# A feature-interaction network on one core: chunk 1's products, the weight splits and chunk 0's loads put in another order

## The reference

```python
prev = x
for k in range(3):
    z = jnp.einsum('bmd,bhd->bdmh', x, prev).reshape(b, D, m * h)
    t = jnp.einsum('bdc,co->bdo', z, ws[k]) + bs[k]
    t = jnp.transpose(t, (0, 2, 1))
    norm = jnp.sqrt(jnp.sum(t * t, axis=(-2, -1), keepdims=True))
    t = t / norm
    logit.append(t)
    prev = t
z = jnp.sum(jnp.concatenate(logit, axis=1), axis=-1)
...
h = jnp.maximum(h @ W_top1 + b_top1, 0.0)
h = jnp.maximum(h @ W_top2 + b_top2, 0.0)
y = h @ W_top3
```

## Time and profile before

| | |
|---|---|
| median of 3 runs | 1050.79 us |
| profiled execution | 1049.29 us |
| its span | 1047.5 us |
| granted TensorE clock, mean of the span | 1.0 |
| TensorE busy | 1019.5 us, 97% |
| VectorE busy | 967.0 us, 92% |
| GpSimd busy | 872.4 us, 83% |
| ScalarE busy | 795.6 us, 76% |
| data moved | 46.10 MB |

### The profile page before, as it was taken

One profiled execution on the slowest core, in us unless ns is written; L12 is line 12 of the kernel. 1 busy time (PEld: TensorE's weight loads), 2 busy tenths in 40 slices (PEclk: granted clock), 3 DMA queues, 4 the chain that ended last, 5 costly groups with the idle time before them and its releaser, 6 DMA issues.

```text
span 1047.5 us, 17976 instructions
## 1 busy us (share of the span) xinstructions
PE 1019.5 (97%) x4322; PEld 786.8 (75%) x4322; DVE 967.0 (92%) x3345; ACT 795.6 (76%) x2655; POOL 872.4 (83%) x729
## 2 busy tenths in 40 slices
PE   2999999999999999999999999999999999999998
PEld 0467777878777787877778787777878777787883
DVE  2589999999999999999999999999999999999993
ACT  3476878878787887878788787878878787888872
POOL 6778989898888989888898989889898887777770
DMA  5540030412103030210303021030302103000000
GB/s 189 132 138 19 4 89 3 97 53 57 36 6 87 3 90 3 49 45 5 88 3 90 2 56 37 4 89 3 90 2 50 42 4 88 1 1 1 2 1 1
DMA packets 75892, 46.10 MB, mean 44 GB/s; under 512 B 55689, under 2 KB 58633, under 8 KB 75658
## 3 DMA queue, kind: packets, MB, share of 16 engines
q1 hardware_dynamic: 68487, 38.59, 15.5%
q10 hardware_dynamic: 2179, 5.07, 1.4%
q0 software_dynamic: 5120, 1.29, 1.4%
HBM read 42.99 MB, written 1.94 MB: 43 GB/s over the span
## 4 chain that ended last, share of the span: by engine, by line
PE 94%; DVE 3%; POOL 1%; issue 1%; DMA 1%; ACT 0%; SPq 0%; DVEq 0%; ACTq 0%
PE bank_d L735 14%; PE bank_d L737 14%; PE bank_d L736 14%; PE bank_a L735 13%; PE bank_a L737 13%; PE bank_a L736 13%; PE acc L795 8%; DVE sums L963 1%; PE turned L778 1%; PE turned L816 1%; POOL gathered L433 1%; PE bank_d L890 1%; PE bank_a L845 1%; PE small L804 0%; DMA base_sb<-in_bases 0%
## 5 line engine op out<-in xcount | busy, mean ns | idle before, releaser
L450 POOL TENSOR_TENSOR sums<-sums,scaled 128x512 f32<-128x512 f32 (+1 forms) x512 | 660.7, 1291 | 113.9 <-ACT scaled L572 79.1
L963 DVE SCALAR_TENSOR_TENSOR sums<-bank_d,x_col,sums 128x128 f32<-128x128 f32 x2304 | 656.5, 339 | 32.5 <-PE bank_d L737 22.4
L572 ACT ACTIVATE scaled<-bank_a,x_col 128x128 f32<-128x128 f32 x1920 | 555.7, 385 | 134.0 <-PE bank_a L737 125.6
L735 PE MATMUL bank_d<-w_hi,prev_lo 128*128 128x512 f32 x640 | 279.0, 436 | 2.2 <-DVE sums L982 2.0
L735 PE MATMUL bank_a<-w_hi,prev_lo 128*128 128x512 f32 (+1 forms) x640 | 269.4, 421 | 2.5 <-issue 1.7
L737 PE MATMUL bank_d<-w_hi,prev_hi 128*128 128x512 f32 x640 | 252.6, 395 | 0.0
L736 PE MATMUL bank_d<-w_lo,prev_hi 128*128 128x512 f32 x640 | 252.4, 394 | 0.0
L737 PE MATMUL bank_a<-w_hi,prev_hi 128*128 128x512 f32 (+1 forms) x640 | 245.4, 383 | 0.0
L736 PE MATMUL bank_a<-w_lo,prev_hi 128*128 128x512 f32 (+1 forms) x640 | 244.8, 383 | 0.0
L572 ACT ACTIVATE sums<-bank_a,x_col 128x128 f32<-128x128 f32 x512 | 146.6, 370 | 65.1 <-PE bank_a L737 64.2
L433 POOL DMA_INDIRECT gathered<-in_table,idx x160 | 168.8, 1055 | 28.2 <-issue 14.7
(11 more groups left out here) (85 smaller groups left out, 537.7 us busy)
## 6 DMA issues: line engine op xcount, KB each, us to landing
x_pairs<-x_scratch SPq DMA_DIRECT2D x135, 156.0 KB
x_pairs<-x_scratch SPq DMA_DIRECT2D x96, 78.0 KB
gathered<-in_table,idx POOLq DMA_INDIRECT x160
x_sq<-x_scratch SPq DMA_DIRECT2D x32, 64.0 KB
x_pairs<-x_scratch SPq DMA_DIRECT2D x92, 22.0 KB
x_scratch<-gathered SPq DMA_DIRECT2D x16, 72.0 KB
w_raw<-in_w ACTq DMA_DIRECT2D x1, 1024.0 KB, 5.2
w_raw<-in_w ACTq DMA_DIRECT2D x1, 896.0 KB
```

Of the source, the lines that this page charges most:

```text
L450: nc.gpsimd.tensor_tensor(out=sums[:, n % SUMS, 0:w, :], in0=sums[:, n % SUMS, 0:w, :], in1=scaled[:, a - 1, 0:w, :], op=ALU.add).then_inc ...
L572: op = nc.scalar.activation(to[:, i, :], bank_a[at % A_RING][:, i * UNITS:(i + 1) * UNITS], ACT.Copy, scale=x_of(c, q, a * PER_BANK + i))
L735: nc.tensor.matmul(to, lo, w_h, start=True, stop=False)
L963: nc.vector.scalar_tensor_tensor(out=taken(n, u) if u in LEFT else total, in0=taken(n, u), scalar=x_of(c, q, A_FIELDS + u), in1=total, op0 ...
```

## The change

The places at which chunk 1's products are made and multiplied move: groups 0 and 1 are made ahead of step 0 as before, with one or two splits of layer 2's low parts in front of each; groups 2 and 3 are made in step 0. Tiles 0 and 1 run in the lead, behind A banks 5 and 6; the others in step 0, one at a place. Two more pieces of layer 2 are rounded by ScalarE ahead of step 0. Chunk 0's partner loads, and the 832 KB part of layer 2's weights, go to SyncE's queue between replicas and columns. One filler is taken away; the columns are transposed behind the sum of squares; one gather more is issued in step 0.

```diff
+LEAD_TILES = {5: [0], 6: [1]}
...
-        _made = []
-        _summed = {(0, 0): [0, 1], (0, 2): [2, 3], (0, 4): [4, 5], (0, 6): [6]}
+        _made = [None, None, (0, 3), (0, 7)]
+        _summed = {(0, 0): [2], (0, 1): [3], (0, 3): [4], (0, 4): [5], (0, 6): [6]}
...
-    PAIRS_AT.update({at: (_c, p) for p, at in enumerate(_made)})
+    PAIRS_AT.update({at: (_c, p) for p, at in enumerate(_made) if at})
...
-GATHERS_BEFORE = 7
+GATHERS_BEFORE = 6
...
-W2_LOADS_FIRST, W2_FIRST = 1, 2
-W2_HIGH_AT = {(1, 1): 2, (1, 2): 3, (2, 1): 4, (2, 2): 5}
-W2_LOW_AT = {(1, 14): 2, (2, 10): 3, (3, 10): 4, (4, 8): 5}
+W2_LOADS_FIRST, W2_LOADS_SECOND = 1, 2
+W2_FIRST, W2_SECOND = 2, 4
+W2_HIGH_AT = {(2, 1): 4, (2, 2): 5}
+W2_LOW_AHEAD = [[0, 1], [2]]
+W2_LOW_AT = {(2, 10): 3, (4, 8): 4, (5, 8): 5}
...
                     sp.wait_ge(x_col_made, c)
+                else:
+
+                    for p in range(1, NP - 1):
+                        load_partners(sp, 0, p)
+                    for part in range(W2_LOADS_FIRST, W2_LOADS_SECOND):
+                        load_raw(sp, 2, part)
                 load_squares(sp, c)
                 if c == 1:
-                    for part in range(W2_LOADS_FIRST, len(W_LOADS[2])):
+                    for part in range(W2_LOADS_SECOND, len(W_LOADS[2])):
                         load_raw(sp, 2, part)
...
-            split_high(2, 0)
-            act.wait_ge(scratch_stored, 48)
-
-            for piece in range(1, W2_FIRST):
+            for piece in range(W2_FIRST):
                 split_high(2, piece)
-            for p in range(1, NP - 1):
-                load_partners(act, 0, p)
             act.wait_ge(bias_loaded, 48)
             square_x(0)
+            for piece in range(W2_FIRST, W2_SECOND):
+                split_high(2, piece)
             finish_squares(0, 0)
...
             pe.wait_ge(scratch_stored, 48)
-            keep_busy(5)
+            keep_busy(4)
...
                 bank_for_act(at)
+                for tile in LEAD_TILES.get(at, []):
+                    pair_matmul(1, tile)
...
                 make_pairs(0, p)
+            sum_squares(0, 0)
             turn_x(0)
-            for piece in range(W2_FIRST):
-                split_low(2, piece)
-            sum_squares(0, 0)
...
             features(0)
-            for p in range(NP):
+            for p, pieces in enumerate(W2_LOW_AHEAD):
+                for piece in pieces:
+                    split_low(2, piece)
                 make_pairs(1, p)
```

## The result

The changed kernel took **1051.84 us** in the median of 20 runs (1049.77 to 1054.83), the kernel before 1047.04 in 20 runs taken with them (1046.12 to 1050.82). The ratio is **1.0040, with a 95% interval of 1.0032 to 1.0047**: slower by 4.2 us by that ratio, which is taken over all runs (4.8 between the two medians), where 1.5 us less was forecast. That lies inside what was called no change (half a per cent) and inside the range in us, but the interval excludes a gain. The 1050.79 of the three runs shown ahead of the change was above this kernel's usual 1047, so my starting point (the middle of 1049.29 and 1050.79) was some 3 us too high and hid part of the miss: that 1051.84 lies inside the range is luck. The profiled execution took 1052.25 us, span 1050.5, against 1049.29 and 1047.5.

The account below looks back on a forecast made before the run. The prediction took back-to-back TensorE matmuls to bound the kernel (busy 97% of the span). Its terms, -0.86 + 0.45 - 1.05, gave about -1.5 us and a forecast of 1048.6 us, range 1045.0 to 1052.0.

Parts of the forecast that it names:

- Part 1: Head, one filler less ahead of the picks: 0.86 us won, bounds 0 and 0.86; replicas landing at 27 to 28.
- Part 2: Head, chunk 0's partner loads behind the replicas on SyncE: cost 0, 1.5 us and more in hand.
- Part 3: Head, 832 KB of weights before x's columns, landing at 34 to 35: cost 0; 0 to 2 us for chunk 1's loads.
- Rival (a): Late loads hold the squares and chunk 1's second group: +0.6 us, 1051.4; chance 0.14.
- Part 4: Splits in front of chunk 1's products ahead of step 0: tile 2 starts later, 0.45 us given back, bounds 0 and 2.
- Part 5: Step 0, product groups 2 and 3 and their squares made there: covered, cost 0.
- Part 6: Steps 1 to 4, piece 2's split gone, pieces 4 and 5 later: 1.05 us won, bounds 0 and 2.6.
- rival (b): All of VectorE's waits go in steps 1 to 4, tile 2 doesn't wait: -3.5 us, 1046.6; chance 0.14.
- The sum: Whole kernel: -0.86 + 0.45 - 1.05 = about -1.5 us, forecast 1048.6 us.

Follow-up runs that it names:

- e7: The kernel before with chunk 0's partner loads on SyncE's queue behind the replicas and one filler less: 1049.73 us, ratio 1.0008.
- e13: The changed kernel, unchanged, run for a third profile: 1049.86 us, ratio 1.0027 to the kernel before.
- e8: e7 plus the weights in front of the columns, ScalarE's splits of pieces 2 and 3 ahead of the squares, `turn_x` behind `sum_squares`: 1050.53 us, ratio 1.0023.
- e10: e9 with low parts of pieces 0 to 2 ahead of `sum_squares`, piece 3 ahead of the second products, none at (2, 10): 1051.11 us, ratio 1.0032.
- e12: The changed kernel, unchanged, run for a second profile: 1050.19 us, ratio 1.0032 to the kernel before.
- e11: The kernel before with only the 832 KB weights' load moved, right behind chunk 0's columns: 1048.66 us, ratio 1.0008.
- e15: The kernel before with the weights early as in e9 and piece 2's split moved between chunk 1's product groups 0 and 1: 1047.81 us, ratio 1.0003.
- e6: The kernel before with only the new places of chunk 1's products and tiles: 1048.18 us, ratio 1.0003.
- e14: The kernel before, unchanged, run for a third profile: 1047.05 us, ratio 1.0000.
- e4: The kernel before with only VectorE's splits of pieces 4 and 5 moved to (4,8) and (5,8): 1049.51 us, ratio 1.0015.
- e2: The changed kernel with VectorE's splits of pieces 4 and 5 back at (3,10) and (4,8): 1050.15 us, ratio 1.0019.
- e3: The changed kernel with ScalarE taking chunk 0's squares and values ahead of the splits that wait for the weights: 1051.15 us, ratio 1.0028.
- e9: The changed kernel with e2's edit and the weights loaded at about 8 us on ScalarE's queue: 1048.91 us, ratio 1.0010.
- e16: As e15, but with the splits of pieces 2 and 3 between chunk 1's product groups: 1052.06 us, ratio 1.0037.
- e5: The changed kernel with e2's and e3's edits and the weights' load behind the columns: 1049.26 us, ratio 1.0010.
- e1: The kernel before, unchanged, run for a second profile: 1047.97 us, ratio 1.0003.

## Why the prediction was wrong

**Part 1 was right in its place, and lost.** The replicas landed at about 27, as forecast (ScalarE's work on them, behind their landing, was over by 28.3). Between profiles with the same number of slow passes (6, 4, 3) the picks came 0.75, 0.61 and 0.93 us earlier than in the kernel before, and e7 has 0.8 us with a whole clock. In two of the three profiles of the kernel after it goes into waiting for the squares: the picks are early, ScalarE is not. And it has a price that I did not see: VectorE's product comes earlier too and can run into the last gather of chunk 1. **Part 2** was 2 us off: I had the last of x's 15 loads land at 31.6, and VectorE had to wait for the third group until 33.50 to 33.62 in three profiles (after, e13, e8), and until 33.27 in e10, which has no weights behind it. There were not 1.5 us in hand; TensorE lost at most 0.2 by it.

**Part 3 is the first step that failed.** "Landing at 34 to 35" was 35.45, 36.3 and 37.05 in the three profiles of the kernel after. Most of that is Part 2's miss, since the weights were to move behind x's loads; for themselves I had given them 2.5 us, at the 341 GB/s of another stretch, and they took 2.8 to 3.5 behind the third group (e13, after) while chunk 1's gathers and x's columns moved beside them. The cover of ScalarE was called the thinnest in the head and costed at 0. By the start of the first bank, between profiles with the same number of slow passes and with the earlier picks counted in, the hold cost nothing in e12, 1.2 us in e13 and 1.5 in the first profile. "Cost 0 to 2 us for chunk 1's loads", value taken 0: the gathers were stored at 36.82, 37.61 and 37.65 and the loads issued from 40.20 to 40.76; the three profiles of the kernel before have 35.64, 36.01 and 37.02, and 38.64, 39.01 and 40.16. In the middle of three that is 1.6 and 1.7 us later. The reason given, SyncE's own issue of the columns, was wrong. That issue does block: it took 5.32 us from 26.94 and 3.12 from 29.81 in e7, and ended at 32.3 and 32.9 (that a full queue blocks it, no row shows). But e11 has the delay with SyncE free. It was the gathers' data, and the last gather's issue.

Rival (a)'s mechanism, late loads that hold the squares and chunk 1's second group, is what happened; I had given it 0.14. Its 1051.4 next to the measured 1051.84 is luck: it priced the whole at +0.6 us on a start that was 3 us too high, and it had no cost for the late splits.

That all queues share the DMA engines is what the Trainium skill says too (DMA: Bandwidth & Descriptors, "Issuing engines are not separate DMA queues"); I had used it for x's loads and not for the gathers that the weights would meet.

**Part 4, "0.45 given back", was about 1.6 us in e12 and 1.7 in e13.** VectorE, from its timeline in e12:

```profile
47.27 2.27 DVE L941 TENSOR_TENSOR z<-x_pairs 128x1024 f32<-128x1024 f32 x1 [1.37 <-DMA x_pairs<-x_scratch]
49.46 2.15 DVE L915 TENSOR_TENSOR w_lo<-w_raw,w_hi 128x896 fp32r<-128x896 f32 x1
51.54 2.02 DVE L941 TENSOR_TENSOR z<-x_pairs 128x1024 f32<-128x1024 f32 x1
```

I took turns of 1.0 to 1.28 us each; three in a row took 2.27, 2.15 and 2.02, since every one of them ran beside GpSimd's adds (four of them in 7.04 us from 45.44). Group 0's loads let it start at 47.27, some 0.3 us behind my plan, and the turns did the rest. So its products ended at 49.54 and not 48.0, and TensorE waited for them (0.98 at 49.68) as well as for group 1's (0.59 at 53.62). The split stands in VectorE's idle time only as long as it takes its own length; e15, with the weights loaded long before, still pays 0.45 for it.
The Trainium skill (SBUF — State Buffer, "Who interferes with whom") has these two kinds of instruction exclude each other. I had named that rule as one that would cost GpSimd and not TensorE; the rows show that it fell on VectorE, with TensorE behind it.

**Part 5** held: e6 costs nothing, groups 2 and 3 took 1.25 and 0.74 us in step 0 and nobody waited for them.

**Part 6, "1.05 won", is the other step that failed**, and here the sign was wrong. The 0.8 in step 2 came. But I bounded the loss by 0 and named "the extra split beside products in step 5" only against rival (b). It measured -1.05 in step 4, +1.4 in step 5, +1.6 in step 6 and -0.5 in step 9 (e12 against e14, e4 the same): +1.5 for the two splits, +0.7 for the part. What I missed is that VectorE's two-input instructions of steps 5 and 6 meet GpSimd's there, as shown with e4 and e10.

**The sum**, with a whole clock: -0.8 (fillers), +2.5 (weights and splits in the head, e8 less e7), +0.1 (places), -0.8 (piece 2), +1.3 (late splits) make +2.3; measured is +3.2. The 0.9 left is about what Part 4's turns cost beyond e8, whose products have no split between them; it was not measured by itself, and with so few executions behind each term it may be no more than their scatter. In the first comparison the changed kernel's ten executions with a whole clock had a median of 1051.30, 4.3 over the kernel before (all 20 executions, whose clocks are not on record); 1.1 us of that did not come again in e12 and e13. The wait at 964 us may be part of it; it stays open.

## What to carry to other kernels

An idle stretch of an engine covers moved work only for the length that the work has there: beside GpSimd's adds a split of 1.0 us was one of 2.0, and what stood behind it moved by two; an instruction of 0.74 us was one of 3.5. A transfer put in front of others must be costed at the rate of the stretch that it enters, and against everything that moves there, indirect gathers included. And where an edit moves less than 5 us of 1000, change one place at a time: here a gain of 0.8 us in step 2, and one of about as much at the picks, were hidden under three costs of 1 to 2 us.

## What the runs showed of the hardware

**ScalarE stands still in the head, in some executions, and the clock can fall behind it.** In the profile of e7 ScalarE was idle for 3.62 us ahead of its first bank of layer 1, where most profiles have 0.76 to 0.80, and TensorE waited 3.5 us for it. The view names "remote" as what it waited for, which is no semaphore of this program. ScalarE's timeline and the windows of e7:

```profile
46.15 1.14 ACT L575 ACTIVATE sums<-bank_a,x_col 128x128 f32<-128x128 f32 x4 [3.62 <-remote]
```

```profile
40.00:46.00 6.00, 3.30 (x10) 1.43 (x8) 3.25 (x10) 0.93 (x3) 3.55 (x5) 1.00 0.72 166
46.00:48.00 2.00, 0.57 (x2) 0.50 (x2) 1.22 (x1) 1.85 (x8) 0.00 (x0) 0.78 0.78 209
48.00:50.00 2.00, 2.00 (x6) 1.31 (x4) 0.00 (x0) 1.23 (x6) 1.27 (x1) 0.50 0.71 216
50.00:52.00 2.00, 1.53 (x6) 0.88 (x6) 1.60 (x1) 1.86 (x8) 1.55 (x2) 0.86 0.60 142
```

TensorE was idle, and then the granted clock fell: it was below whole from 46 to 52, and at 0.50, which is the level of 1.2 GHz, from 48 to 50. Like idle times of ScalarE, at its first or second bank, stand in the profiles of e2 (2.78 us), e4 (1.80), e3 (1.06) and e9 (1.07), and in none of the other profiles. The clock stayed whole in e2 and e9; in e4 it was down for some 3 us, in e3 at 0.50 from 46 to 52.

A mean clock below 1.000 has more than one source: in e16 it is the wait of step 6, with the clock at 0.57 from 110 to 114, and e10 has that wait as well. With these two left out, the kernels fall into two groups. Those with chunk 0's partner loads on SyncE's queue and one filler less (the kernel after, e2, e3, e5, e7, e8, e9, e12, e13) had it in 52 of 102 executions, the others (the kernel before, e1, e4, e6, e11, e14, e15) in 44 of 206. So this part of the change seems to double the number of such executions, and e7's gain of 0.8 us with a whole clock is not a gain on average. Whether it is the order of the loads or the filler was not tested apart, and the chips differ: on that of e12 to e14 the kernel before had none in 27. The cause stays open.

**A gather's issue is held by a VectorE product.** The issue of chunk 1's last gather on GpSimd started between 33.5 and 34.0 us in every profile. In eleven of the 18 a product of VectorE with two inputs in SBUF was running by then and had 0.4 us or more to go; there the issue took 1.29 to 1.96 us and ended 0.8 us behind the end of that product: at 35.54 behind 34.75 in the kernel after, at 35.64 behind 34.84 in e1. In the other seven it took 0.92 to 1.02. One of these, e14, fits badly: by the records the product started 0.03 us ahead of the gather, and it was the product that took longer (1.29 instead of 1.22). This shifts the store of chunk 1's gathers by up to 1 us between executions of the same kernel.

**One VectorE instruction can be held by several of GpSimd.** In step 6 of e10 and e16 one VectorE instruction took 3.47 us where it took 0.74 in step 0 of e12, beside three GpSimd instructions in a row of 1.3 to 1.5 us each.
